# A pair-interaction tower on one Trainium2 core: eight more units of products are folded in half, by accumulating transfers that Pool issues between its gathers, and folded batches are summed two slots later

## The reference, cut to what matters

```python
e = stack([tbl_f[ids[:, f]] for f in range(40)], axis=1)   # 512 x 40 x 64
viW = einsum('bpd,pde->bpe', e[:, i_idx], W)
z = einsum('bpe,bpe->bp', viW, e[:, j_idx])                # 512 x 780
h = relu(concat([z, dense]) @ W_top1 + b_top1)
h = relu(h @ W_top2 + b_top2)
y = h @ W_top3
```

## Time and profile before

| | |
|---|---|
| median of three runs | 344.07 us |
| lowest, highest | 342.62, 344.12 us |
| the profiled execution, its own time | 344.23 us |
| its span in the trace | 342.4 us |
| granted TensorE clock | 1.00 throughout |

### The profile page before, as it was taken

One profiled execution on the slowest core, in us unless ns is written; L12 is line 12 of the kernel. 1 busy time (PEld: TensorE's weight loads), 2 busy tenths in 40 slices (PEclk: granted clock), 3 DMA queues, 4 the chain that ended last, 5 costly groups with the idle time before them and its releaser, 6 DMA issues.

```text
span 342.4 us, 5226 instructions
## 1 busy us (share of the span) xinstructions
PE 327.8 (96%) x1622; PEld 113.5 (33%) x1622; DVE 267.7 (78%) x254; ACT 200.1 (58%) x1140; POOL 218.4 (64%) x172
## 2 busy tenths in 40 slices
PE   7888979999999998999999999999999899999997
PEld 3243233333333332333233323333333233233342
DVE  3988799787887878888998998878989869879030
ACT  1454723333132689458999986659967738656131
POOL 5666456646555654557896789889977697676000
PEclk9999999999999999999999999999999999999999
DMA  7745321312312222021851220203203000000000
GB/s 187 271 151 185 99 79 19 113 23 80 113 42 61 82 53 83 15 81 44 277 164 39 85 88 0 79 12 100 75 1 109 17 0 2 0 1 0 2 1 0
DMA packets 11325, 24.25 MB, mean 71 GB/s; under 512 B 3601, under 2 KB 4369, under 8 KB 11170
## 3 DMA queue, kind: packets, MB, share of 16 engines
q1 hardware_dynamic: 7058, 19.72, 17.5%
q0 software_dynamic: 4096, 4.20, 6.0%
q10 hardware_dynamic: 144, 0.00, 0.0%
HBM read 23.91 MB, written 0.00 MB: 70 GB/s over the span
## 4 chain that ended last, share of the span: by engine, by line
PE 76%; ACT 9%; POOL 6%; DMA 4%; issue 3%; DVE 2%; SPq 0%; POOLq 0%
PE u L625 36%; PE zp L646 16%; PE u L613 6%; PE u L682 4%; ACT prod L511 4%; POOL gath L446 4%; PE xp L589 3%; PE xp L660 3%; ACT xq_part L495 3%; POOL prod L454 2%; PE xp L572 2%; PE u L721 2%; DMA gath<-in_tbl,ids_sb 2%; PE u L602 2%; DMA late<-in_small 1%
## 5 line engine op out<-in xcount | busy, mean ns | idle before, releaser
L784 DVE TENSOR_TENSOR prod<-u,xq_part 128x1024 f32<-128x1024 f32 x148 | 173.9, 1217 | 29.9 <-PE u L625 27.3
L446 POOL DMA_INDIRECT gath<-in_tbl,ids_sb x128 | 124.3, 971 | 80.4 <-DMA gath<-in_tbl,ids_sb 47.2
L625 PE MATMUL u<-xt,w_ring 64*128 64x512 f32 x632 | 160.5, 616 | 3.7 <-ACT xt L489 2.5
L511 ACT ACTIVATE prod<-prod 128x64 f32<-128x64 f32 x512 | 122.7, 242 | 22.9 <-DVE prod L765 14.6
L454 POOL TENSOR_TENSOR prod<-prod 128x1024 f32<-128x1024 f32 x40 | 94.0, 2370 | 16.8 <-DVE prod L784 16.6
L511 ACT ACTIVATION_READ_ACCUMULATOR prod<-prod 128x1 f32 x512 | 96.2, 188 | 0.9 <-issue 0.9
L625 PEld LDWEIGHTS u<-xt,w_ring 64*128 64x128 f32 x632 | 54.0, 185 | 96.2 <-issue 48.5
L646 PE MATMUL zp<-prod,sel_sb 128*32 128x512 f32 x492 | 63.4, 600 | 1.6 <-POOL prod L454 1.6
L495 ACT ACTIVATE xq_part<-xt 32x512 f32<-32x512 f32 x72 | 45.2, 627 | 1.8
L765 DVE TENSOR_TENSOR prod<-u,gath 128x1024 f32<-128x1024 f32 x32 | 38.9, 1216 | 4.7 <-PE u L613 4.7
L489 ACT ACTIVATE xt<-xp 128x512 f32<-128x512 f32 x20 | 11.9, 593 | 51.7 <-PE xp L572 36.8
(11 more groups left out here) (39 smaller groups left out, 113.9 us busy)
## 6 DMA issues: line engine op xcount, KB each, us to landing
w_ring<-in_w_cell SPq DMA_DIRECT2D x20, 512.0 KB
late<-in_ids_small SPq DMA_DIRECT2D x4, 512.0 KB, 4.9
gath<-in_tbl,ids_sb POOLq DMA_INDIRECT x128
wide_w<-in_w_wide SPq DMA_DIRECT2D x8, 256.0 KB
late<-in_w_top SPq DMA_DIRECT2D x1, 1792.0 KB, 9.6
late<-in_small SPq DMA_DIRECT2D x3, 512.0 KB
late<-in_small SPq DMA_DIRECT2D x2, 256.0 KB
late<-in_w_top SPq DMA_DIRECT2D x1, 512.0 KB, 8.9
```

The source lines that it names most:

```text
L446: pool.indirect_dma_start(gath[:, place, t, half, :], None, tables[f], bass.IndirectOffsetOnAxis(ap=ids_sb[:, t, f:f + 1], axis=0),).then_ ...
L511: total = act.activation(part, part, ACT.Copy, accum_out=zw_sb[:, t, 2 * HF * j + pair:2 * HF * j + pair + 1])
L625: mm = pe.matmul(u[:, n % UR, a, :], w_ring[rows, q % RW, at * P:(at + 1) * P], xt[rows, moving % XR, :], start=True, stop=True)
L784: dve.tensor_tensor(prod[:, n % PR, :, :], u[:, n % UR, :, :], x, ALU.mult).then_inc(prod_ready, 1)
```

## The change

Blocks 8 to 11 (pairs 4 and 5 in `FOLDED`) get two folded batches each: units (8,2), (8,3), (9,2), (9,3), (10,2), (11,0), (11,3), (11,4), batches 11, 13, 16 and 18. These eight folds are not tensor adds of Pool but transfers with `accum_op` add, from the HI place of the ring to the LO place, 512 KB each, issued from Pool, with four semaphores in turn. `FOLDS_AFTER` is rewritten: one after each half of block 10, two after the first half of block 11, one after each half of blocks 12 and 13; Pool's own folds then start one after the second half of block 14 and five after the first half of block 15. `FOLD_LAG` goes from 10 to 12 for all folded batches. `sum_batch` waits for each folded unit, by its transfer's semaphore or by Pool's count.

```diff
-FOLDED = {6:3,7:4,8:6,9:7}
-FOLDS_AFTER = [0]*22+[2,4,0,3,4,3,3,6,0,0]
+FOLDED = {4: 2, 5: 2, 6: 3, 7: 4, 8: 6, 9: 7}
+DMA_BELOW = 6
+FOLDS_AFTER = [0] * 12 + [1, 1, 2, 0, 1, 1, 1, 1, 0, 1, 5, 0, 1, 3, 4, 3, 5, 2, 0, 0]
...
+DMA_FOLDS = [u for u in FOLDS if u[0] < 2 * DMA_BELOW]
+POOL_FOLDS = [u for u in FOLDS if u[0] >= 2 * DMA_BELOW]
+FR = 4
...
-FOLD_LAG = 10
+FOLD_LAG = 12
...
             def fold(k, q):
                 lo, hi = AT["unit", k, q, LO], AT["unit", k, q, HI]
-                pool.wait_ge(prod_ready, max(DONE[lo], DONE[hi]))
+                if (k, q) in DMA_FOLDS:
+                    i = DMA_FOLDS.index((k, q))
+                    if i >= FR:
+                        pool.wait_ge(dma_folded[i % FR], 16 * (i // FR))
+                    pool.wait_ge(prod_ready, DONE[hi])
+                    pool.dma_start(prod[:, lo % PR, :, :], prod[:, hi % PR, :, :],
+                                   accum_op=ALU.add).then_inc(dma_folded[i % FR], 16)
+                    return
+                pool.wait_ge(prod_ready, DONE[hi])
                 pool.tensor_tensor(prod[:, lo % PR, :, :], prod[:, lo % PR, :, :], prod[:, hi % PR, :, :],
-                                   ALU.add).then_inc(folded, 1)
+                                   ALU.add).then_inc(pool_folded, 1)
...
-                if is_folded:
-                    pe.wait_ge(folded, FOLDS.index(units[-1]) + 1)
+                for unit in units if is_folded else []:
+                    if unit in DMA_FOLDS:
+                        i = DMA_FOLDS.index(unit)
+                        pe.wait_ge(dma_folded[i % FR], 16 * (i // FR + 1))
+                    else:
+                        pe.wait_ge(pool_folded, POOL_FOLDS.index(unit) + 1)
```

More of the change, by code:

```diff
@@ L356, in program @@
         prod_ready = sem("prod_ready")
-        folded = sem("folded")
+        pool_folded = sem("pool_folded")
+        dma_folded = [sem(f"dma_folded{r}") for r in range(FR)]
         summed = sem("summed")
```

## The result

Over 22 runs each the changed kernel took 341.17 us in the median and the kernel before 343.63. Five of the changed kernel's runs, at 343.7 us and above, count as slow and are left out of the ratio, which is 0.9922 with a 95% interval of 0.9904 to 0.9940, that is 2.7 us less (2.1 to 3.3); with all runs the medians differ by 2.5. Forecast were 2.5 us less. The profiled execution took 340.10 us with a span of 338.3.

What follows compares the result with a forecast made beforehand. TensorE was taken to set the end on average, VectorE in stretches without sums. Terms -4.35 - 2.4 + 4.2 - 0.6 + 0.6 = -2.5 us took 344.23 to 341.7, median 341.6 us; range 340.5 to 348.3.

Steps and rivals of the forecast that it cites:

- The lag: FOLD_LAG 10 to 12: TensorE's one wait for Pool's folds falls from 0.7 to 0.1 us, -0.6 us.
- The lumps: Sums gathered in 33 places, not 40: TensorE saves 0.91 and 2.4 us, waits for VectorE add 4.2.
- What the transfers give: Four batches lose their second round on TensorE, -3.44 us, against +0.6 us of item 11's wait.
- The waits for VectorE: TensorE's waits for VectorE products, over all slots, grow from 4.7 to 8.9 us: +4.2.
- The places named by hand: TensorE's timeline: fill 47 ends and item 10 forms at 105.3 us, item 12 at 136.5, item 18 at 255.
- Its issue: Pool's issue of one adding transfer: 1.25 us, from an indirect transfer's 0.95 plus 0.3; bounds 0.95 and 2.5.
- T: Time of one adding transfer on the 16 DMA engines: taken as 4 us, between 1.6 and 8.9.
- Item 11's wait: Block 11's second-half gather, behind two transfers, lands at 118.7 us; item 11 stood at 118.2: wait 0.6 us.
- The one wait for Pool falls to 0.1: TensorE's only wait for a Pool fold, at the sum near 272 us, falls from 0.7 to 0.1 us.
- B: Rival, slower: long adding transfers delay block 11's gather; +4.0 us (348.1) at 6 us per transfer. Chance 0.19.
- C: Rival, slower: each transfer's issue costs Pool 2.5 us, item 11 waits over 3 us; +2.2, 346.3 us. Chance 0.08.
- D: Rival, no change: VectorE takes back TensorE's savings, or transfers take 4.4 to 5.4 us; -1.7 to +1 us. Chance 0.23.

Runs made afterwards that it cites:

- e9: The changed kernel itself run again, on a third chip, against the kernel before: ratio 0.9922.
- e1: The kernel before with FOLD_LAG 12 in place of 10 and nothing else, no transfers: ratio 0.9953 against the kernel before.
- e5: The kernel before with FOLD_LAG 12 and batches 11, 13, 16, 18 left plain but summed at the change's later slots, no transfers: ratio 1.0000 against before.
- e7: The changed kernel with the fold of (8,3) moved back, so three transfers precede block 11's second-half gather: ratio 1.0010 against the kernel before.
- e3: The changed kernel with its eight early folds done as Pool tensor adds instead of transfers: ratio 0.9980 against the kernel before.
- e6: The changed kernel without the eight adding transfers, result incomplete, for timing only: ratio 0.9916 against the kernel before.

## Why the prediction was right, step by step

**The total**: -2.5 forecast, -2.7 measured, and about 2 at equal clock (e9: 1.8 and 2.4). It is right in part by luck, since two terms were too small and cancel. The lag I had at -0.6 in the sum (-0.9 as forecast for e1), and it brought 1.6 by the ratio and 1.8 to 2.3 at equal clock. The lumps, -0.91 - 2.4 + 4.2 = +0.9 in the sum, cost 1.6 by the ratio and 2.3 to 2.4 at equal clock (e5 against e1). What the transfers give, -3.44 + 0.6 = -2.8 in the sum, was 2.7 by the ratio and 2.4 at equal clock (changed kernel against e5), at equal clock no more than the lumps took. The profiled execution gained more, 344.23 - 340.10 = 4.1 us: 0.8 of it was there before item 9 was formed, and 1.2 is the unexplained gap of the kernel before at 129.85. Neither is the change's.

**Second rounds and lumps.** The 32 records are gone (460, not 492). A lump of x24 takes 142.50 - 139.79 = 2.71 us again, one of three batches 3.56, so the prices hold. That the lumps would be paid back in waits for VectorE was the claim hardest to see in a profile; e5 tests it alone and finds 1.0000 where TensorE's own ledger says 3.3 us less. The direction is shown, the size was larger than forecast.

**The waits for VectorE** I had put at +4.2. The view of waits can't check this number: the weight loads' idle time before a product of VectorE rises from 33.3 to 45.4 us, but most of it lies behind matmuls that are still under way. The places named by hand come out: 8.04 us for the eight fills from 96.69 (forecast 7.8), item 10 at 104.73 in a trace that was 0.8 early (forecast 105.3), item 12 at 135.22 (136.5), item 18 at 255.54 (255).

**The adding transfer.** Its issue alone is 0.98 to 1.02 us, as the indirect one that I took it from; two in a row take 1.93, without the gap of 0.3. Its time T was taken as 4 us. Two of them ahead of block 11 give (119.0 - 1.85 - 108.5) / 2 = 4.3; the same two in e9 give 3.8 and three in e7 give 3.4. Of engine time it is 2.9, which is 1.8 times the plain piece's 1.6. The Trainium skill's rule (Collectives: The Full Stack, section "The bandwidth ceiling: the fold count and why AG ≠ RS ≠ AR"), half the rate of a copy because of the second read, is stated there for ring transfers between ranks; the estimate by its 31 GB/s per engine was 2.1 us. Half the rate fits this case roughly, 2.9 against 1.6; the 31 GB/s does not, since the plain piece moved 0.52 MB / (16 x 1.6 us) = 20 GB/s per engine.

**Item 11's wait**, the tightest place: 0.6 forecast, 1.01 found in one trace of the changed kernel and none in the other (e9), and 2.30 in e3 where an add of Pool stands for each issue. That what stands ahead of the gather sets its landing is shown by the landing waits: 4.32 and 3.19 us behind two transfers, 4.92 behind three (e7). The wait of TensorE itself is only 0 to 1 us.

**Pool's lateness was forecast too small.** "The one wait for Pool falls to 0.1": in the trace two waits stand, 0.69 at 169.15 and 0.42 at 272.18, 1.1 in total (in e9 even 1.96 and 0.48). The prediction walked Pool's list up to block 12 and looked again only at the sum near 272 us. In between, the sum in slot 94 needs Pool's first two tensor adds. Before, they ended at 162.8, 6.6 us ahead of that sum (then in slot 92, at 169.42); now the second one starts behind the first gather of block 15, at 166.64, ends at 169.0, and the sum follows at 169.15.

**The rivals.** B's mechanism is real (the landing waits above); it didn't come to its threshold, since T was 3.4 to 4.3 and B begins above 4.4. Its price, 2 us for each us of T, was not tested. C fell with an issue of 1.0 us. D's mechanism, VectorE taking back what TensorE saves, is what e5 shows; at equal clock it ate as much as the missing second rounds gave (2.3 to 2.4 against 2.4), and the gain left is no larger than the lag's.

What stays open: the 1.0 to 1.3 us gaps in which TensorE and VectorE both seem to wait, and whether the changed kernel, as it stands, is faster than the lag alone; the two were not run on one chip.

## What to carry to other kernels

An accumulating transfer can take an add off a busy engine for the price of its issue, but it shares its queue with every gather behind it: count how many stand ahead of the one gather that is due next, and put the others after it. Look at the whole list behind it too: here the order of one transfer moved Pool's own adds, 40 us later, by 3.7 us. When a batch's work is deferred, its neighbours that must keep the order are deferred with it, and the lump starves the engine that was fed in between; price the move on both engines, slot by slot. And when a result comes through a slower path, the slack of its consumer has to grow first: here the later sums alone gave 1.6 us of the 2.7, if not all of it, the transfers without them nothing, and the transfers with one of them moved some 1.5 us more.

## What the runs showed of the hardware that I had not expected

Two accumulating transfers issued back to back cost Pool 1.93 us, three 2.79: 0.97 and 0.93 each, while indirect transfers have 0.3 us between them. The first gather issued behind such a transfer takes 1.05 to 1.07 us instead of 0.95. Eight transfers with 23 us of engine time beside the weight pieces cost no more than about 1.4 us (e6). And a wait of TensorE can cost more than itself: after 2.30 us of standing in e3 and 1.87 at 174.47 in e7 the granted clock was at 0.50 for some 3.3 us, which cost 1.6 us each time; after 1.96 us in e9 and 2.34 at 114.30 in e7 it stayed at 1.00.
